# Normalisations taken in two chunks: centring, squares and sums chunk by chunk, in a one-core vision-transformer kernel

## The chip, the cores and the metric

One core of one Trainium2 chip runs the whole program in a single launch. The metric is the device time of that launch in microseconds; each kernel is run several times and the median is compared.

## The reference

The network is two small transformer layers over 16 images of 37 tokens (592 tokens) with 256 features. The kernel keeps everything transposed: features on the 128 partitions in C = 2 chunks, tokens along the free axis, in two halves of 296 tokens (HALF).

```python
def _layernorm(x, axis=-1, eps=1e-05):
    m = jnp.mean(x, axis=axis, keepdims=True)
    v = jnp.var(x, axis=axis, keepdims=True)
    return (x - m) / jnp.sqrt(v + eps)
...
h = _L0_tok_ref(...)                       # patch embedding
h = h + _L0_attn_ref(_layernorm(h), ...)   # two attentions, each behind an RMS norm
h = h + _L0_ffn_ref(_layernorm(h), ...)    # router, 32 experts, 2 shared experts
h = h + _L1_attn_ref(_layernorm(h), ...)   # third attention
h = h + _L1_ffn_ref(_layernorm(h), ...)    # int8-like FFN, scales from the largest |weight|
```

## The kernel before

There is no compiler scheduling: each engine (PE for matmuls, DVE for vector work, ACT for activations, POOL for GpSimd work, SP for DMA) has its own instruction list in the source and runs it strictly in order. Engines meet only at semaphores, so a wait holds everything behind it on that engine.

The norms are numbered. Norm 0 stands in front of the first attention, norm 1 (an RMS norm over the stream x0 of the first block) between the first and second attention, norm 2 in front of the experts, norm 3 in front of the third attention; the last one has code of its own.

Norms 0, 2 and 3 share one scheme. PE multiplies h by a matrix of 1/256 (two chunks summed in a PSUM bank, L1271 is the matmul helper) and gets the mean, each half in a bank. DVE subtracts it (`centre`, L887), one instruction for both chunks of a half. ACT squares xc (`norm`, L597), one instruction for a half, behind whatever stands ahead in its list. PE sums the squares into the variance (`norm`, L1271). ACT takes a table reciprocal root (L600) and squares it (L602). DVE corrects it with one Newton step and applies it (`norm_apply`: L896, L898, L901). POOL, in norms 0 and 1, multiplies by the norm's weights beside this (`norm_weighted`, L449). BUSY holds the numbers of filler matmuls (bf16, results unused) that PE issues ahead of the mean, between mean and variance, and after the variance.

Norm 1 is spread out. DVE adds the attention's output to x0 (`stream_added`, L992), ACT squares it (`stream_squares`, L607), PE sums it (`stream_variance`), ACT takes the root (`stream_rsqrt`, L612, L614), DVE does `norm_apply(1, ...)`. The first half goes in front of the second attention's projections. The second half is worked off inside `qk_units(1)`: this is a pipeline of six units (query and key projections of a half each), with the rotary products on DVE (rb L938, ra L941), their sum and scaling on POOL (L460, L464), head norms on PE and ACT (L658, L661), and the last product on DVE (L948, L952). On DVE the second half's `norm_apply` stands behind the rotary products of unit 0. On PE the projection of unit 3 waits for the second half of xn and for the rotary products of unit 0, whose PSUM bank it reuses.

In front of norm 2, SP loads the first four experts (L390) after the last attention scores, and ACT rounds each (L723, `high_part`) ahead of norm 2's squares in its list. DVE reads the largest weights of the last FFN in eight parts (`weight_peak`, L907) wherever it has time, the last of them and their combination (`weight_peaks`, L913) in front of `centre(2)`.

Of the kernel before, what the change touches and what calls it, by code (L numbers as in the profile page):

```python
# [11 lines left out]
P = 128  # L12
# [27 lines left out]
LN_EPS, RMS_EPS = 1e-5, 1e-6  # L40

START_BUSY = 19
BUSY = ((7, (0, 4, 14)), (0, (5, 0, 10)), (3, (0, 0, 8)), (7, (6, 4, 14)), (3, (5, 4, 10)))
LEAD = 3
ATTENTION_BUSY = 5

# [37 lines left out]
def program(nc, x, w_lin, consts, consts_bf, vecs, g_wq, g_down, g_k, g_v, g_wo, l_wq, l_wk, l_wv, l_wo,  # L84
# [4 lines left out]
    with ExitStack() as ctx:  # L89
# [169 lines left out]
        s_mean = sem("mean_summed")  # L259
        s_cent = sem("tokens_centred")  # L260
        s_sq = sem("squares_ready")
        s_var = sem("variance_summed")
        s_ars = sem("table_rsqrt_ready")
        s_xw = sem("tokens_weighted")
# [86 lines left out]
        def cent_count(n, hf):  # L351

            return 2 * {0: 0, 2: 1, 3: 2, 4: 3}[n] + hf + 1

        def score_bank(a, p):

            return 4 + 2 * (p % 2) if a < 2 else 6
# [73 lines left out]
        def _(pool):  # L431
# [8 lines left out]
            def norm_weighted(n, weight, factor):  # L440

                src = x0 if n == 1 else xc
                for hf in range(2):
                    if n == 1:
                        pool.wait_ge(s_x0, hf + 1)
                    else:
                        pool.wait_ge(s_cent, cent_count(n, hf))
                    for c in range(C):
                        ins = nc.gpsimd.tensor_scalar(xn[:, c, half(hf)], src[:, c, half(hf)],  # L449
                                                      weight[:, c:c + 1], -0.5 * factor, ALU.mult, ALU.mult)  # L450
                    ins.then_inc(s_xw, 1)
# [101 lines left out]
        def _(act_e):  # L553
# [29 lines left out]
                warmed[0] += 1  # L583
                nc.scalar.activation(spare[:, k:k + 1], eps[:, 0:1], func)  # L584

            def norm(n, mean=True, eps_at=0):

                if n != 2:
                    load_table(ACT.Abs_reciprocal_sqrt)
                for hf in range(2):  # L590
                    if mean:
                        act_e.wait_ge(s_cent, cent_count(n, hf))
                        src = xc
                    else:
                        act_e.wait_ge(s_x0, hf + 1)
                        src = x0
                    nc.scalar.activation(sq[:, :, half(hf)], src[:, :, half(hf)], ACT.Square).then_inc(s_sq, 1)  # L597
                for hf in range(2):
                    act_e.wait_ge(s_var, 2 * n + hf + 1)
                    link(nc.scalar.activation(ars[:, half(hf)], ps[2 + hf][:, 0:HALF], ACT.Abs_reciprocal_sqrt,  # L600
                                              bias=eps[:, eps_at:eps_at + 1]))
                    nc.scalar.activation(nt[:, half(hf)], ars[:, half(hf)], ACT.Square).then_inc(s_ars, 1)  # L602

            def stream_squares(hf):

                act_e.wait_ge(s_x0, hf + 1)
                nc.scalar.activation(sq[:, :, half(hf)], x0[:, :, half(hf)], ACT.Square).then_inc(s_sq, 1)  # L607

            def stream_rsqrt(hf):

# [261 lines left out]
        def _(dve):  # L872
# [11 lines left out]
            def centre(n):  # L884
                for hf in range(2):
                    dve.wait_ge(s_mean, cent_count(n, hf))
                    nc.vector.tensor_tensor(xc[:, :, half(hf)], h[:, :, half(hf)],  # L887
                                            bc(ps[hf][:, 0:HALF].unsqueeze(1), [P, C, HALF]), ALU.subtract)\
                        .then_inc(s_cent, 1)

            def norm_apply(n, count, eps_at=0, halves=range(2)):

# [32 lines left out]
            def qk_units(a):  # L925
                names = (("cos_g", "sin_g"), ("cos_l", "sin_l"))[a]
                cos, sin = (bc(const(x).unsqueeze(1), [P, HB, S]) for x in names)

                def images(ap):
                    return ap.rearrange("p (b s) -> p b s", s=S)  # L930

                for u in range(NPROJ + 1):
                    n = a * NPROJ + u
                    if u < NPROJ:
                        dve.wait_ge(s_swap, n + 1)
                        if n >= 2:
                            dve.wait_ge(s_rsum, n - 1)
                        nc.vector.tensor_tensor(images(rb[:, u % 2, :]), images(ps[5 + 2 * (u % 2)][:, 0:HALF]), sin,  # L938
                                                ALU.mult)
                        dve.wait_ge(s_qsq, n + 1)  # L940
                        nc.vector.tensor_tensor(images(ra[:, u % 2, :]), images(ps[PROJ_BANKS[u % 3]][:, 0:HALF]), cos,  # L941
                                                ALU.mult).then_inc(s_rope, 1)
                    if u >= 1:
                        w, k = u - 1, (u - 1) % 2
                        dve.wait_ge(s_qars2, n)

                        t = ps[MEAN_BANKS[w]][:, 0:HALF]
                        link(nc.vector.scalar_tensor_tensor(t, t, eps[:, 2:3], rs2[:, k, :], ALU.add, ALU.mult))  # L948
                        dve.wait_ge(s_rscaled, n)
                        j, hf = QK_UNITS[w]  # L950
                        dst = qt[:, j, half(hf)] if j < 2 else sq[:, 0, half(hf)]
                        ins = nc.vector.scalar_tensor_tensor(dst, t, -3.0, rt[:, k, :], ALU.add, ALU.mult)  # L952
                        ins.then_inc(s_qk, 1)
                    if u >= 2 and QK_UNITS[u - 2][0] == 2:

                        hf = QK_UNITS[u - 2][1]
                        for g in range(ACT_VARIANTS, 4):
                            ins = nc.vector.tensor_scalar(km[:, 0, g, half(hf)], sq[:, 0, half(hf)],  # L958
                                                          const("onehot4")[:, g:g + 1], None, ALU.mult)
                        ins.then_inc(s_kmv, 1)  # L960
                    if a == 1 and u == 0:
                        norm_apply(1, 4, 2, (1,))

            def normalise_grouped(a, p):

# [22 lines left out]
            def stream_added(hf):  # L988

                dve.wait_ge(s_wo, hf + 1)  # L990
                dve.wait_ge(s_x0s, hf + 1)
                nc.vector.tensor_tensor(x0[:, :, half(hf)], x0[:, :, half(hf)],  # L992
                                        psum[:, 2 - 2 * hf:4 - 2 * hf, 0:HALF], ALU.add).then_inc(s_x0, 1)

            nc.vector.memset(zeros[:], 0.0).then_inc(s_zero, 1)
            for k in range(KT):
# [25 lines left out]
            for a in range(2):  # L1022
# [21 lines left out]
                for hf in range(2):  # L1044
# [6 lines left out]
                    if hf == 0:  # L1051
                        weight_peak(1, 1)
                        weight_peak(1, 2)
                    else:
                        weight_peak(1, 3)
                        weight_peaks()


            centre(2)
            norm_apply(2, 6)  # L1060
            for hf in range(2):
                dve.wait_ge(s_xh, hf + 1)
# [206 lines left out]
        def _(pe):  # L1269
# [6 lines left out]
                for _ in range(count):  # L1276
                    mm(ps[bank][:, 0:HALF], lhsT, rhs, True, True)

            def norm(n, mean=True):

                spare_bank, busy = BUSY[n]
                if n:
                    keep_busy(spare_bank, busy[0])
                if mean:
                    for hf in range(2):
                        pe.wait_ge(s_h, cent_count(n, hf))
                        if n == 3:
                            pe.wait_ge(s_hd, hf + 1)
                        for c in range(C):
                            ins = mm(ps[hf][:, 0:HALF], const("mean"), h[:, c, half(hf)], c == 0, c == C - 1)  # L1290
                        ins.then_inc(s_mean, 1)
                    spare_bank = 7
                    keep_busy(spare_bank, busy[1])
                for hf in range(2):
                    pe.wait_ge(s_sq, 2 * n + hf + 1)
                    for c in range(C):
                        ins = mm(ps[2 + hf][:, 0:HALF], const("mean"), sq[:, c, half(hf)], c == 0, c == C - 1)
                    ins.then_inc(s_var, 1)
                keep_busy(spare_bank, busy[2])
# [43 lines left out]
            def qk_units(a):  # L1343
                projection(a, 0)
                for u in range(NPROJ):
# [5 lines left out]
                        pe.wait_ge(s_qk, a * NPROJ + 3)  # L1351
                        value_sums(a, 0)
                    if a == 1 and u == 0:
                        pe.wait_ge(s_x0, 2)
                        stream_variance(1)
                    exchange(a, u)
                    head_mean_squares(a, u)
# [108 lines left out]

            def stream_variance(hf):

                pe.wait_ge(s_sq, 2 + hf + 1)
                for c in range(C):  # L1470
                    ins = mm(ps[2 + hf][:, 0:HALF], const("mean"), sq[:, c, half(hf)], c == 0, c == C - 1)
                ins.then_inc(s_var, 1)

# [69 lines left out]
            def last_attention():  # L1543
# [25 lines left out]
                pe.wait_ge(s_cb, 2)  # L1569
                for m in range(C):  # L1570
                    mm(ps[4 + m][:, 0:HALF], const("ident"), xc[:, m, half(1)], True, False)
                pe.wait_ge(s_sq, 9)
                for c in range(C):
                    ins = mm(ps[6][:, 0:HALF], const("mean"), sq2[:, c, :], c == 0, c == C - 1)
                ins.then_inc(s_var, 1)
# [2 lines left out]
                for m in range(C):  # L1578
                    centred_projection(1, m, True)
                for c in range(C):  # L1580
                    pe.wait_ge(s_sq, 10 + c)
                    ins = mm(ps[7][:, 0:HALF], const("mean"), rs2[:, c, :], c == 0, c == C - 1)
                ins.then_inc(s_var, 1)
                plain_projection(0)
# [70 lines left out]
                for hf in range(2):  # L1655
                    mm(ps[2 * m + hf][:, 0:HALF], const("ident"), h[:, m, half(hf)], True, False)

            pe.wait_ge(s_cent, cent_count(2, 1))
            seed(0)
            pe.wait_ge(s_moe_w, 48)  # L1660
            pe.wait_ge(s_xn, 5)
# [270 lines left out]
```

## Time and profile before

| | us |
|---|---|
| median of 3 runs | 364.17 (363.68 to 365.55) |
| the profiled execution, whole | 365.47 |
| its span, first to last instruction | 363.6 |
| PE busy | 344.2 (95%) |
| DVE, ACT, POOL busy | 233.5, 196.1, 137.5 |

The span is the profile's; 1.87 us of the profiled execution lie around it. Each engine's busy time says how full it is on the whole; which of them sets the time at a place is read from the chain of work that ended last and from the idle time in front of an instruction.

### The profile page before, as it was taken

Reading aid. Unit: us, or ns where it says so; the run is one execution under the profiler, and the core shown is the slowest. Engines: PE = TensorE matmul, PEld = TensorE weight load, DVE = VectorE, ACT = ScalarE, POOL = GpSimd, SP = SyncE. Lnnn points to the kernel's source line nnn. Section 1 sums busy time; section 2 is a strip of 40 time slices with the busy share of each in tenths; the row PEclk is TensorE's granted clock in tenths of the full one; section 3 lists DMA queues with packets and bytes.
Section 4 is the critical chain, followed back from the end, with each engine's and each line's share of the span. In section 5 each row is a group of like instructions: output and inputs, shape, how many; then the busy total and the mean of one; then the engine's idle time right before and its main releaser. Section 6 shows DMA issues by size and latency. Waiting matters only on the chain.

```text
span 363.6 us, 9925 instructions
## 1 busy us (share of the span) xinstructions
PE 344.2 (95%) x3935; PEld 295.8 (81%) x3935; DVE 233.5 (64%) x512; ACT 196.1 (54%) x392; POOL 137.5 (38%) x145
## 2 busy tenths in 40 slices
PE   7999899898988999999999999999999999999994
PEld 6856667686657989999999999999999678676653
DVE  4656788897859466555555555555557464666687
ACT  5267943786464344445445444544543786425772
POOL 0046761472250256555666544444440002341000
PEclk9999999999989999999999999999999999999999
DMA  8930000000560244454444455444500000000001
GB/s 289 399 148 1 3 5 31 1 4 4 170 179 2 57 139 135 156 154 143 127 137 142 139 153 153 126 140 138 147 19 2 0 0 4 4 6 2 3 0 67
DMA packets 14865, 32.08 MB, mean 88 GB/s; under 512 B 2480, under 2 KB 4464, under 8 KB 14576
## 3 DMA queue, kind: packets, MB, share of 16 engines
q1 hardware_dynamic: 13328, 30.48, 26.6%
q10 hardware_dynamic: 1504, 1.13, 0.9%
q8 instruction: 24, 0.39, 0.4%
q14 instruction: 9, 0.07, 0.1%
HBM read 30.91 MB, written 0.69 MB: 87 GB/s over the span
## 4 chain that ended last, share of the span: by engine, by line
PE 76%; DVE 9%; ACT 8%; issue 2%; DMA 2%; ACTq 1%; SPq 1%; POOL 1%; DVEq 0%
PE psum L1271 76%; DMA km<-in_experts 2%; ACT L584 1%; DVE xn L901 1%; ACT region L855 1%; ACTq L563 1%; DVE km L1197 1%; ACT ah L744 1%; ACT region L679 1%; SPq L390 1%; DVE nt L898 1%; DVE nt L896 1%; ACT e L691 1%; ACT sq L597 1%; DVE rt L1126 1%
## 5 line engine op out<-in xcount | busy, mean ns | idle before, releaser
L1271 PE MATMUL psum<-xh,split_all 128*128 128x296 f32 x544 | 122.1, 299 | 0.0
L501 POOL TENSOR_TENSOR split_all<-km,split_all 128x768 fp32r<-128x768 f32 x34 | 62.6, 1844 | 81.3 <-ACT split_all L723 81.3
L1271 PEld LDWEIGHTS psum<-xh,split_all 128*128 128x128 f32 x544 | 91.6, 188 | 0.1
L1271 PE MATMUL psum<-xl,split_all 128*128 128x296 f32 (+1 forms) x288 | 85.4, 301 | 0.3 <-POOL xl L544 0.3
L744 ACT ACTIVATE ah<-rt 128x296 fp32r<-128x296 f32 x64 | 28.9, 452 | 72.7 <-DVE rt L1126 65.9
L1271 PEld LDWEIGHTS psum<-xl,split_all 128*128 128x128 f32 (+1 forms) x288 | 53.3, 187 | 1.2 <-issue 0.5
L1271 PE MATMUL psum<-ah,split_all 128*128 128x296 f32 x272 | 48.7, 300 | 1.7 <-ACT ah L744 1.6
L1128 DVE TENSOR_TENSOR al<-rt,ah 128x296 fp32r<-128x296 f32 x60 | 28.1, 468 | 31.0 <-ACT ah L744 31.0
L1123 DVE TENSOR_TENSOR rb<-psum,wb 128x296 f32<-128x296 f32 x60 | 28.0, 466 | 25.3 <-ACT psum L742 25.3
L1271 PEld LDWEIGHTS psum<-ah,split_all 128*128 128x128 f32 x272 | 40.6, 188 | 2.7 <-ACT ah L744 2.1
L1126 DVE TENSOR_TENSOR rt<-rb,psum 128x296 f32<-128x296 f32 x60 | 27.8, 463 | 4.8
L742 ACT ACTIVATE psum<-psum 128x296 f32<-128x296 f32 x60 | 24.1, 401 | 12.0 <-PE psum L1271 11.9
L723 ACT ACTIVATE split_all<-km 128x768 fp32r<-128x768 f32 x34 | 28.3, 833 | 3.8 <-DMA km<-in_experts 3.7
L1271 PE MATMUL psum<-al,split_all 128*128 128x296 f32 x136 | 30.0, 301 | 0.2
L691 ACT ACTIVATE e<-psum 101x592 f32<-101x592 f32 x24 | 15.7, 663 | 21.9 <-PE psum L1271 21.7
L544 POOL TENSOR_TENSOR xl<-mx,cst 128x592 fp32r<-128x592 f32 x8 | 9.6, 1202 | 45.0 <-DVE mx L1206 45.0
L1271 PEld LDWEIGHTS psum<-al,split_all 128*128 128x128 f32 x136 | 22.1, 189 | 0.9 <-POOL al L507 0.5
L1271 PE MATMUL psum<-cstb 128*128 128x296 bf16 (+1 forms) x174 | 21.4, 297 | 0.5 <-DVE km L958 0.3
L1271 PE MATMUL psum<-sq,cst 128*128 128x296 f32 x60 | 20.0, 453 | 1.9 <-ACT sq L597 1.8
L971 DVE RECIPROCAL rc<-psum 128x148 f32<-128x148 f32 x16 | 17.3, 1083 | 5.3 <-PE psum L1271 4.1
L1271 PEld LDWEIGHTS psum<-cstb 128*128 128x128 bf16 (+1 forms) x174 | 12.6, 100 | 8.7 <-issue 5.2
L1271 PEld LDWEIGHTS psum<-sq,cst 128*128 128x128 f32 x60 | 11.8, 204 | 6.8 <-ACT sq L597 3.5
(225 smaller groups left out, 578.6 us busy)
## 6 DMA issues: line engine op xcount, KB each, us to landing
km<-in_experts SPq DMA_DIRECT2D x34, 384.0 KB, 4.1
wb<-weights SPq DMA_DIRECT2D x32, 296.0 KB, 3.8
w_sb<-in_w SPq DMA_DIRECT2D x2, 1024.0 KB, 8.5
region<-in_x SPq DMA_DIRECT2D x6, 296.0 KB, 4.8
region<-in_w_lin ACTq DMA_DIRECT2D x6, 128.0 KB, 5.2
qkv_sb<-in_qkv_w SPq DMA_DIRECT2D x1, 768.0 KB, 4.8
cst<-in_consts SPq DMA_DIRECT2D x1, 502.5 KB, 7.1
out<-x SPq DMA_DIRECT2D x2, 148.0 KB, 1.8
```

The lines of the kernel that those rows point to most:

```text
L390: sp.dma_start(ring[i], experts[i, :, :]).then_inc(s_ring[i], 16)
L501: nc.gpsimd.tensor_tensor(wl[i], ring[i], wh[i].bitcast(f32), ALU.subtract)\
L544: nc.gpsimd.tensor_tensor(dg[:, p % 2, :, :], mx[:, p % 2, :].unsqueeze(2).broadcast_to([P, HEADS, S]), const("minus_ident").unsqueeze(1). ...
L691: nc.scalar.activation(e[0:ROWS, p % 2, 0:EC].rearrange("p (k n) -> p k n", k=2), psum[0:ROWS, sb0:sb0 + 2, 0:HALFPOS * S], ACT.Exp, scale ...
L723: nc.scalar.activation(wh[i], ring[i], ACT.Copy).then_inc(s_wsh, 1)
L742: nc.scalar.activation(gate, ps[bank][:, 0:HALF], ACT.Silu).then_inc(s_sg, 1)
L744: nc.scalar.activation(ah[:, j, :], act[:, j, :], ACT.Copy).then_inc(s_ah, 1)
L971: link(nc.vector.reciprocal(rc[:], bank[:, G4 * S:2 * G4 * S]))
L1123: nc.vector.tensor_tensor(gu[:, j, :], gate, weight, ALU.mult).then_inc(s_mulc, 1)
L1126: nc.vector.tensor_tensor(act[:, j, :], gu[:, j, :], ps[5][:, 0:HALF], ALU.mult).then_inc(s_act, 1)
L1128: nc.vector.tensor_tensor(al[:, j, :], act[:, j, :], ah[:, j, :].bitcast(f32), ALU.subtract)\
L1271: return nc.tensor.matmul(out_, lhsT, rhs, start=start, stop=stop, skip_group_check=True)
```

## The change

The centring, the squares and the sums of squares of norms 0, 2 and 3 are split by chunk: DVE issues two subtractions of 296 columns for each half and signals each; ACT squares each chunk as it is signalled, under a semaphore of its own; PE waits for each chunk ahead of its matmul. The same is done with the addition, squares and sums of norm 1. The POOL steps that read both chunks wait for the second. The fillers between mean and variance go from 4 to 2 in norms 0 and 3. The last `weight_peak` and `weight_peaks` go behind `centre(2)` on DVE. The second half's `norm_apply` of norm 1 goes in front of unit 0's rotary products on DVE. No arithmetic is changed.

```diff
-BUSY = ((7, (0, 4, 14)), (0, (5, 0, 10)), (3, (0, 0, 8)), (7, (6, 4, 14)), (3, (5, 4, 10)))
+BUSY = ((7, (0, 2, 14)), (0, (5, 0, 10)), (3, (0, 0, 8)), (7, (6, 2, 14)), (3, (5, 4, 10)))
...
+        def chunk_count(n, hf, c):
+            return C * (cent_count(n, hf) - 1) + c + 1
...
@@ norm_weighted, POOL
-                        pool.wait_ge(s_x0, hf + 1)
+                        pool.wait_ge(s_x0, C * (hf + 1))
-                        pool.wait_ge(s_cent, cent_count(n, hf))
+                        pool.wait_ge(s_cent, chunk_count(n, hf, C - 1))
...
@@ norm, ACT
-                    nc.scalar.activation(sq[:, :, half(hf)], src[:, :, half(hf)], ACT.Square).then_inc(s_sq, 1)
+                    for c in range(C):
+                        act_e.wait_ge(s_cent, chunk_count(n, hf, c))
+                        nc.scalar.activation(sq[:, c, half(hf)], xc[:, c, half(hf)], ACT.Square).then_inc(s_sqc, 1)
...
@@ stream_squares, ACT
-                act_e.wait_ge(s_x0, hf + 1)
-                nc.scalar.activation(sq[:, :, half(hf)], x0[:, :, half(hf)], ACT.Square).then_inc(s_sq, 1)
+                for c in range(C):
+                    act_e.wait_ge(s_x0, C * hf + c + 1)
+                    nc.scalar.activation(sq[:, c, half(hf)], x0[:, c, half(hf)], ACT.Square).then_inc(s_sq, 1)
...
@@ centre, DVE
-                    nc.vector.tensor_tensor(xc[:, :, half(hf)], h[:, :, half(hf)],
-                                            bc(ps[hf][:, 0:HALF].unsqueeze(1), [P, C, HALF]), ALU.subtract)\
-                        .then_inc(s_cent, 1)
+                    for c in range(C):
+                        nc.vector.tensor_tensor(xc[:, c, half(hf)], h[:, c, half(hf)], ps[hf][:, 0:HALF], ALU.subtract)\
+                            .then_inc(s_cent, 1)
...
@@ qk_units, DVE
+                    if a == 1 and u == 0:
+                        norm_apply(1, 4, 2, (1,))
                     if u < NPROJ:
                         dve.wait_ge(s_swap, n + 1)
...
-                    if a == 1 and u == 0:
-                        norm_apply(1, 4, 2, (1,))
...
@@ stream_added, DVE
-                nc.vector.tensor_tensor(x0[:, :, half(hf)], x0[:, :, half(hf)],
-                                        psum[:, 2 - 2 * hf:4 - 2 * hf, 0:HALF], ALU.add).then_inc(s_x0, 1)
+                for c in range(C):
+                    nc.vector.tensor_tensor(x0[:, c, half(hf)], x0[:, c, half(hf)], ps[2 - 2 * hf + c][:, 0:HALF], ALU.add)\
+                        .then_inc(s_x0, 1)
...
@@ end of the second attention, DVE
-                    else:
-                        weight_peak(1, 3)
-                        weight_peaks()
             centre(2)
+            weight_peak(1, 3)
+            weight_peaks()
             norm_apply(2, 6)
...
@@ norm, PE
                 for hf in range(2):
-                    pe.wait_ge(s_sq, 2 * n + hf + 1)
                     for c in range(C):
+                        pe.wait_ge(s_sqc, C * (cent_count(n, hf) - 1) + c + 1)
                         ins = mm(ps[2 + hf][:, 0:HALF], const("mean"), sq[:, c, half(hf)], c == 0, c == C - 1)
...
@@ stream_variance, PE
-                pe.wait_ge(s_sq, 2 + hf + 1)
                 for c in range(C):
+                    pe.wait_ge(s_sq, C * hf + c + 1)
```

## Rows read from the trace of the kernel before

**Rows 1.** The page: busy time of PE, and the chain's shares by engine

```profile
PE 344.2 (95%) x3935; PEld 295.8 (81%) x3935; DVE 233.5 (64%) x512; ACT 196.1 (54%) x392; POOL 137.5 (38%) x145
...
PE 76%; DVE 9%; ACT 8%; issue 2%; DMA 2%; ACTq 1%; SPq 1%; POOL 1%; DVEq 0%
```

**Rows 2.** Chain that ended last, whole span: start us, us, what

```profile
17.95 0.78 DVE xc L887
18.75 0.70 ACT sq L597
...
69.50 9.47 PE psum L1271 x92
...
95.45 6.13 DMA km<-in_experts
...
133.56 139.14 PE psum L1271 x1020
...
285.33 0.78 DVE xc L887
...
286.89 1.28 PE psum L1271 x4
```

**Rows 3.** Timeline, norm 0: start, us, engine, line, instruction, count [idle before]

```profile
18.74 0.67 PE L1271 MATMUL psum<-cstb 128*128 128x296 bf16 x4
...
19.50 2.26 PE L1271 MATMUL psum<-sq,cst 128*128 128x296 f32 x8
```

**Rows 4.** Timeline: pairs of 296-column instructions, on ACT and on DVE

```profile
5.49 0.77 ACT L574 ACTIVATE split_all<-region 128x296 fp32r<-128x296 f32 x2
...
96.78 0.83 DVE L1049 TENSOR_TENSOR h<-h,psum 128x296 f32<-128x296 f32 x2
```

**Rows 5.** Timeline, norm 1, weight loads of PE: the first half's sums

```profile
57.00 0.97 PEld L1271 LDWEIGHTS psum<-vec,outw_sb 128*128 128x128 f32 x8 [0.24 <-issue]
58.01 0.80 PEld L1271 LDWEIGHTS psum<-sq,cst 128*128 128x128 f32 x4
```

**Rows 6.** Timeline, second attention's first units: ACT, DVE, POOL and PE

```profile
66.08 0.47 DVE L938 TENSOR_TENSOR rb<-psum,cst 128x296 f32<-128x296 f32 x1 [1.38 <-PE psum L1271]
66.12 0.45 ACT L614 ACTIVATE nt<-ars 128x296 f32<-128x296 f32 x1
66.46 0.46 DVE L941 TENSOR_TENSOR ra<-psum,cst 128x296 f32<-128x296 f32 x1
67.00 0.82 POOL L460 TENSOR_TENSOR rt<-ra,rb 128x296 f32<-128x296 f32 x1 [2.99 <-DVE ra L941]
...
67.90 0.92 POOL L464 TENSOR_TENSOR rt<-rt,rs 128x296 f32<-128x296 f32 x1
68.18 1.27 DVE L901 TENSOR_TENSOR xn<-xn,nt 128x592 f32<-128x592 f32 x1
69.50 1.26 PE L1271 MATMUL psum<-xn,lk_sb 128*128 128x296 f32 x4 [0.97 <-DVE xn L901]
```

**Rows 7.** Timeline, norm 0's Newton step: first and last of three instructions

```profile
21.83 0.53 DVE L896 SCALAR_TENSOR_TENSOR nt<-psum,eps,nt 128x296 f32<-128x296 f32 x1 [2.11 <-ACT nt L602]
...
22.89 0.77 DVE L901 TENSOR_TENSOR xn<-xn,nt 128x592 f32<-128x592 f32 x1
```

**Rows 8.** Timeline, norm 2

```profile
100.66 1.79 ACT L723 ACTIVATE split_all<-km 128x768 fp32r<-128x768 f32 x2 [1.40 <-DMA km<-in_experts]
100.78 1.44 DVE L887 TENSOR_TENSOR xc<-h,psum 128x592 f32<-128x592 f32 x2
102.36 1.27 ACT L597 ACTIVATE sq<-xc 128x592 f32<-128x592 f32 x2
103.09 3.95 PE L1271 MATMUL psum<-sq,cst 128*128 128x296 f32 x8 [1.78 <-ACT sq L597]
```

**Rows 9.** Stretches of norm 2: us, busy times, granted clock, DMA share, GB/s

```profile
103.42:106.84 3.42, 3.42 (x8) 2.18 (x7) 0.60 (x2) 1.16 (x3) 1.74 (x1) 0.50 0.77 200
```

**Rows 10.** Timeline, PE: the longest idle time at full clock elsewhere

```profile
44.27 0.46 PE L1271 MATMUL psum<-e,region 101*32 101x74 f32 x16 [1.07 <-ACT e L691]
```

## What I predicted before the change was run

> **What bounds the kernel now.** I read the shares of busy time first: PE is at work for 344.2 us of a span of 363.6, and the chain that ended last runs over PE for 76% of it [rows 1]. So nearly every stretch is already PE's. What the change can win lies in the places where the chain leaves PE, and the second view is therefore the chain in order of time. It leaves PE in each norm. In norm 0 it goes from DVE's centring (0.78 us) to ACT's squares (0.70) and back to PE's sums at 19.50 [rows 2, 3], and in norm 3 in the same way [rows 2]. In norm 2 it comes from the DMA of the fourth expert (6.13 us) over ACT [rows 2, 8]. In norm 1 the first half's sums follow another PE job without a gap [rows 5], while the second half ends in a PE idle time of 0.97 us that DVE's xn ended [rows 6]. The third view is the timeline at those four places, to see for each engine what it was doing when its operand became ready. The fourth is the granted clock, because one stretch is not at full clock [rows 9].
>
> **Norm 0: chunks and two fillers fewer.** Now, PE starts summing squares at 19.50, which is 17.95 + 0.78 + 0.70 and hand-overs. No row shows the chunked instructions, so I take rows of the same shape: a pair of DVE instructions of 296 columns with a PSUM operand takes 0.83, so one is ready after 0.47 and the second is offset by 0.36; a pair of SBUF copies on ACT takes 0.77, so one takes 0.45 and the offset is 0.32 [rows 4, 6]. The first chunk is centred at 17.95 + 0.47 = 18.42, squared from 18.45 to 18.90, and PE could take it at 18.94. PE itself is then still at its fillers. Four of them occupied 18.74 to 19.41, of which the last 0.17 or so is the drain of the last, so that one fills about 0.125 [rows 3]; with two, the next matmul can be issued at 18.99. PE starts at 18.99 and not 19.50: 0.50 less. With four fillers left in, it would have been 19.24 and half that gain. The second chunk: centred by 17.95 + 0.83 = 18.78, squared by 19.26, wanted by PE half a half-sum later, at 19.49. It's in time. The second half's mean is read at 18.95, so its chunks are squared at about 19.90 and 20.22, and wanted at 19.99 and 20.49: PE goes through all eight pieces (2.26 us [rows 3]) without a gap. The whole 0.50 reaches the end, since the following root, Newton step and projection hang on these sums. Bounds: 0.25 (if PE's change from filler to sum takes the time of the two fillers) and 0.55 (both instructions cut to a chunk: 0.78 + 0.70 - 0.47 - 0.45 = 0.56). I take 0.50, because the PE slot is the later of the two.
>
> The costs of splitting are 0.06 on DVE for each half (0.83 against 0.77) and 0.07 on ACT (0.77 against 0.70) [rows 4, 8]. POOL's weighting waits for the second chunk and starts 0.06 later; its product is used two microseconds after it is done, so I cost it at nothing. If that cover were gone it would be the 0.06.
>
> The Trainium skill speaks against such a split: "VectorE: DVE Perf Modes", section "The TRN2 errata", says that instructions reading SBUF pay a fixed extra latency each, and advises tiles of at least 512 elements. By that rule all six halves of norms 0, 2 and 3 would pay 0.13 us, 0.8 in all, and the sum would be a gain of about 0.7. The trace agrees that a fixed cost exists (0.83 against 0.77), but the chain only waits for the first chunk.
>
> **Norm 3** repeats norm 0: from the start of the centring (285.33) to the first sum (286.89) it takes 1.56 [rows 2], where norm 0 takes 1.55, with the same instructions and the same four fillers. Gain 0.50, same bounds.
>
> **Norm 1, first half.** The squares would be ready about 0.55 earlier, but PE isn't. It loads weights for the output bias from 57.00 to 57.97 and starts the sums at 58.01 [rows 5]. The gain is the 0.04 between the two, called 0. The second half's squares are overtaken by PE's projections in the same manner. DVE's 0.06 goes into a wait for ACT. I cost this part at nothing; bounds -0.04 and +0.06.
>
> **Norm 1, Newton in front of unit 0.** Today DVE does rb and ra of unit 0 (66.08 to 66.92), then the Newton step, and xn is ready at 69.45, so that PE starts unit 3's projection at 69.50 [rows 6]. The last of its three instructions takes 1.27, against 0.77 in norm 0, and the three together 2.6 (66.83, behind ra, to 69.45) against 1.83 there (21.83 to 23.66) [rows 6, 7]. They ran while POOL did unit 0's sum and scaling (67.00 to 68.82), which ra released. Moved in front, the Newton step waits for ACT's root (66.12 + 0.45 = 66.57; this is the added wait, and unit 0's rb, which was ready at 66.08, is queued behind it). It then runs with POOL idle: 66.60 + 1.83 = 68.43. So xn is ready 1.02 earlier. But that isn't what PE gets, because the next wait is late: unit 3's projection also needs ra of unit 0, whose bank it takes. rb and ra follow at 68.35 and 68.72 and end at 69.18. PE starts at 69.22 and not 69.50: 0.28. Who else waits for the held rb? POOL's sum of unit 0 starts at 69.26 instead of 67.00, and POOL needs 0.9 + 0.9 for each unit. I followed the queues through: POOL ends unit 0 at 70.96, unit 1 at 72.75 (before 71.97), unit 2 at 74.53 (73.93), unit 3 at 76.32 (75.93). DVE's last product of unit 0 ends at 71.46 (71.14), of unit 1 at 73.25 (73.09), of unit 2 at 75.03, of unit 3 ahead of before. PE's head sums of unit 3 need unit 0's product, at 72.8, and those of unit 4 unit 1's, at 74.8. Each has more than a microsecond. From 69.50 on, the chain is PE's for 9.47 us [rows 2], so the 0.28 is carried. Bounds: 0 (POOL's delay reaches PE) and 0.35 (the hand-over shorter). A loss is bounded by the delay of DVE's product, 0.3.
>
> **Norm 2.** Here ACT is the gate, not DVE. Its two last expert roundings end at 102.45 and the squares follow at 102.36 (issue overlaps), while the centring was through at 101.5 and 102.22 [rows 8]. Moving the last weight peak behind the centring makes centring some 0.5 earlier and changes nothing, because ACT only comes when the fourth expert has landed at 101.58 [rows 2]. If the DMA were earlier in another run, the peaks' 0.7 would come in; I give this 0 to 0.2. The peaks themselves are wanted far later, after the fillers behind the sums. Chunking: first square ready at 102.36 + 0.45 + 0.04 = 102.85 where PE now starts at 103.09: 0.24. The expert loads start after the last scores and so move along with the gains ahead of them. Bounds 0 and 0.3, without the clock.
>
> **The sum.** 0.50 + 0 + 0.28 + 0.24 + 0.50 = 1.52 us. The profiled execution takes 365.47 (span 363.6 and 1.87 around it), so it would become 363.95. On the median of the runs, 364.17, the same 1.52 gives 362.65. The profiled execution is 1.3 slower than that median, and norm 2 has a reason for it, below. After norm 2, PE's stretch through the experts is one piece of the chain (139.14 us [rows 2]), so nothing there takes the gain back.
>
> **Rivals.**
> *The clock in norm 2.* In the trace PE's granted clock is 0.50 (1.2 instead of 2.4 GHz) from 103.42 to 106.84, behind an idle time of 1.78 us, and the eight pieces of the sums take 3.95 us where norm 0's take 2.26 [rows 3, 8, 9]: 1.69 us lost on the path. An idle time of 1.07 elsewhere was not followed by a fall [rows 10]. The change makes the idle time 1.54, between the two. If the clock then stays up, the profiled execution would end at 363.95 - 1.69 = 362.3, and a median that had the fall in it would come to about 361.0. The fastest run before, 363.68, is 1.79 below the profiled one, which is about one fall; so the fall is probably not in every run, and part of the median is free of it already. The Trainium skill, "TensorE: Matmul & The Clock Gate", section "What's actually happening", has it that the half rate is the default and activity releases it, and that the moment varies between runs. By that rule the shorter idle time would make falls rarer, and the trace agrees in direction. Time 361.4, chance 0.25.
> *The fillers were holding the clock.* Two fillers fewer in norms 0 and 3: PE is less active there, and the clock falls in one of them as it does in norm 2. Its price is up to 1.69 each, so 362.65 + 1.69 = 364.3 for one and 366.0 for both. This is slower than before. It decides as soon as one fall comes there; against it speaks that by my schedule PE is idle for only about 0.1 around the fillers. Chance 0.05.
> *The chunks pay nothing.* If the hand-over for each chunk costs more than the rows show (PE now waits four times instead of twice), or the fixed costs lie on the path, each norm gives 0.1 to 0.2: 364.17 - 0.28 - 0.5 = 363.4. Chance 0.13.
> *The unit pipeline takes the Newton gain back.* POOL begins unit 0 2.3 us later. If its backlog reached PE's head sums, norm 1 would lose up to 0.3 instead of gaining 0.28: 363.2. Chance 0.12.
> The forecast has the rest, 0.45. That the change does not do what it says is in the third rival.
>
> **How the numbers follow.** Forecast 362.6. The low end is the clock rival's, 361.0; the high end goes over the third and fourth rival and a fall kept in more runs, 364.0. A change of 0.5% is 1.82 us, about what a measurement of this kernel can tell from none. That bound is at 362.35, just 0.3 beyond the forecast, so the forecast's own chance is shared: of its 0.45 about a third lies beyond. Faster by over 0.5%: 0.15 + 0.25 = 0.40. Slower by over 0.5%: 0.03, from both falls. Within: 0.57.
>
> **What would show it.** Right: PE's first sum of squares 0.50 nearer to the start of the centring in norms 0 and 3, with no idle time among the eight pieces; xn L901 of the second half at 0.77 instead of 1.27 and PE's unit 3 released by ra L941, 0.28 nearer to the root; in norm 2 sums starting 0.4 us after the fourth rounding. Wrong: an idle time of PE between chunks; POOL as releaser inside units 3 to 5; a granted clock of 0.5 in norms 0 or 3; or the centring as the last releaser in norm 2.

## The result, and the profile after

The change took 2.0 us: median 362.10 us of 17 runs against 364.55 us of 17 runs of the kernel before on the same chips, ratio 0.9945 with a 95% interval of 0.9928 to 0.9962 (1.4 to 2.6 us). The 2.0 is taken from this ratio; the two medians by themselves differ by 2.45. The forecast was 362.6, a gain of 1.52. In a second set the same changed kernel gave 0.9939 [0.9916, 0.9962]. Single slow executions of the later sets (423 us and more: two of newton_only, one of after_busy2, one of the kernel before in each group) are left out of every ratio.

The profiled execution of the changed kernel took 360.44, its span is 358.6. That is 5.0 less than the span of before, more than twice the measured gain, so most of what two single traces differ by isn't the change. The page of the changed kernel, busy time by engine (here PE is as full as in [rows 1]):

```profile
span 358.6 us, 9933 instructions
PE 342.3 (95%) x3931; PEld 294.7 (82%) x3931; DVE 233.3 (65%) x520; ACT 197.1 (55%) x400; POOL 137.2 (38%) x145
```

Eight instructions more on DVE and eight more on ACT, four fewer on PE (two fillers in each of two norms). The chain that ended last, changed kernel (start us, us, what), at the places of [rows 2]:

```profile
19.12 0.47 DVE xc L890
19.62 0.82 ACT sq L598 x2
20.44 0.51 ACT ars L601
...
68.21 0.38 DVE ra L945
68.59 0.14 issue
68.73 9.44 PE psum L1273 x92
...
94.14 5.03 DMA km<-in_experts
99.19 0.84 ACT split_all L725
100.04 0.35 ACT sq L598
...
129.94 138.20 PE psum L1273 x1020
...
281.72 0.47 DVE xc L890
282.21 0.82 ACT sq L598 x2
```

In norms 0 and 3 the chain now goes from a centring of one chunk over ACT's squares straight to ACT's root: these are the squares of the second half, and the root of the first half stands behind them in ACT's list. PE's sums are no longer on it. Unit 3's projection is released by ra. Norm 2 still hangs on the DMA and ACT's rounding. The expert loop took 138.20 in this trace and 139.14 in [rows 2], though nothing in it was changed. Of the fourteen profiles this one and newton_only have 138.20, the other twelve 139.12 to 139.14; a second profile of the same changed kernel (after_again) has 139.12.

The timeline of norm 0 in the changed kernel, to be held against [rows 3]:

```profile
18.12 0.83 DVE L890 TENSOR_TENSOR xc<-h,psum 128x296 f32<-128x296 f32 x2 [0.67 <-PE psum L1273]
18.62 0.82 ACT L598 ACTIVATE sq<-xc 128x296 f32<-128x296 f32 x2 [5.12 <-DVE xc L890]
18.92 0.42 PE L1273 MATMUL psum<-cstb 128*128 128x296 bf16 x2
...
19.18 2.21 PE L1273 MATMUL psum<-sq,cst 128*128 128x296 f32 x8
```

The first sum starts 1.06 after the centring (1.55 before), and the eight pieces run without idle time. In norm 3 the same distance is 281.77 - 280.72 = 1.05.

To separate the change from what merely differs between executions, I cut all fourteen profiles of this study at the same instructions. The columns: norm 0's centring to the first projection; the bias job to norm 1's first projection; ACT's root to unit 3's projection; the first expert's DMA to norm 2's first sum; that sum to the expert loop; norm 3's centring to its projection. The last column is the stretch from there to the last FFN, in which no kernel differs. All are differences of starts, in us.

```
                    norm0  norm1  root-u3  load-sum2  sum2-loop  norm3  rest
before               5.86   5.31    3.92      9.99      30.47     5.77  52.02
newton_only          5.86   5.32    3.75      9.71      29.33     5.77  52.17
peaks_only           5.86   5.32    3.93      9.21      29.36     5.76  53.08
before_busy2         5.86   5.32    3.92      9.53      29.37     5.77  53.70
before_fillers2      5.86   5.31    3.92      9.51      29.36     5.78  52.72
after                5.31   5.20    3.75      8.81      29.51     5.22  52.16
after_again          5.30   5.20    3.75      8.67      29.60     5.21  52.45
chunks_only          5.30   5.32    3.91      9.35      29.50     5.21  52.18
after_fillers4       5.51   5.20    3.75      8.57      29.70     5.41  51.75
after_busy2          5.31   5.20    3.76      9.04      29.26     5.21  52.95
after_stream_back    5.30   5.31    3.75      8.80      29.37     5.21  52.47
after_peaks_back     5.31   5.20    3.75      8.64      29.71     5.21  51.63
after_newton_back    5.30   5.20    3.92      9.36      29.50     5.21  52.47
after_round_late     5.30   5.21    3.75      8.62      30.47     5.21  52.70
```

Four columns repeat to 0.02 and move only with their own part of the change. The others vary from one profile to the next, the last one by 2 us (51.63 to 53.70) over code that is the same in all. A gain of a tenth can be read in the first kind of column, while the medians can't show it.

### The profile page after: what moved, and what is told of

Its sections match the earlier page's. It is cut to its first block, busy times and chain, and to the rows that moved or that the text cites. A ratio compares the mean times of both kernels' runs of the same rounds, so it can differ in the third digit from the quotient of the medians.

```text
span 358.6 us, 9933 instructions
## 1 busy us (share of the span) xinstructions
PE 342.3 (95%) x3931; PEld 294.7 (82%) x3931; DVE 233.3 (65%) x520; ACT 197.1 (55%) x400; POOL 137.2 (38%) x145
## 4 chain that ended last, share of the span: by engine, by line
PE 78%; DVE 8%; ACT 8%; issue 2%; DMA 1%; ACTq 1%; SPq 1%; POOL 0%; DVEq 0%
PE psum L1273 78%; DMA km<-in_experts 1%; DVE xn L903 1%; ACT region L857 1%; DVE nt L898 1%; DVE nt L900 1%; ACTq L568 1%; ACT L589 1%; SPq L395 1%; DVE km L1199 1%; ACT region L681 1%; ACT e L693 1%; ACT sq L598 1%; DVE rt L1128 1%; ACT ah L746 1%
## 5 line engine op out<-in xcount | busy, mean ns | idle before, releaser
L1273 PE MATMUL psum<-cstb 128*128 128x296 bf16 (+1 forms) x170 | 20.6, 297 | 0.3 <-DVE km L962 0.3
L1273 PE MATMUL psum<-sq,cst 128*128 128x296 f32 x60 | 18.2, 417 | 0.3 <-ACT sq L598 0.3
L465 POOL TENSOR_TENSOR rt<-ra,rb 128x296 f32<-128x296 f32 x12 | 9.9, 825 | 15.1 <-DVE ra L945 15.1
```

The source lines that it names most:

```text
L465: nc.gpsimd.tensor_tensor(rt[:, u % 2, :], ra[:, u % 2, :], rb[:, u % 2, :], ALU.add)\
L1273: return nc.tensor.matmul(out_, lhsT, rhs, start=start, stop=stop, skip_group_check=True)
```

## The experiments

Each kernel was timed in five rounds beside the kernel before, in three groups, each on one chip: chunks_only, newton_only, peaks_only and after_fillers4; before_busy2, after_busy2, after_round_late and after_stream_back; after_again, after_peaks_back, after_newton_back and before_fillers2.

**chunks_only.** The change without norm 1's chunks, without the Newton move and without the move of the peaks:

```diff
-BUSY = ((7, (0, 4, 14)), ... (7, (6, 4, 14)), ...)
+BUSY = ((7, (0, 2, 14)), ... (7, (6, 2, 14)), ...)
 # centre, norm (ACT and PE) and norm_weighted by chunk, as in the change
```

> Of the change only the centring, squares and sums by chunk in norms 0, 2 and 3, with the two fillers fewer; norm 1, the Newton step and the weight peaks stay as before. My theory: PE's first sum of squares comes 0.5 us nearer to the start of the centring in norms 0 and 3 (from 1.55 to about 1.05), 0.24 nearer in norm 2; 1.2 to 1.3 us less in all, ratio about 0.9965, plus what the clock gives back in norm 2. Rival (the Newton step or the peaks carry much of the measured 2.0): this kernel gains under 0.8 us.

Measured: 0.9968 [0.9950, 0.9986], 1.2 us, as forecast. The interval runs from 0.5 to 1.8 us and so doesn't exclude the rival's 0.8 by itself; the table does it, with 0.56 for norm 0 and 0.56 for norm 3.

**newton_only.** The kernel before with `norm_apply(1, 4, 2, (1,))` in front of unit 0:

```diff
+                    if a == 1 and u == 0:
+                        norm_apply(1, 4, 2, (1,))
                     if u < NPROJ:
...
-                    if a == 1 and u == 0:
-                        norm_apply(1, 4, 2, (1,))
```

> Only the second half's Newton step of norm 1 moved in front of unit 0. My theory, corrected by the trace of the changed kernel: PE's projection of unit 3 starts 0.17 us nearer to ACT's root than before (3.75 instead of 3.92), released by ra and not by xn; no time that a median can show, ratio 0.9990 to 1.0000. Rival (the move carries the surplus of the measured gain): at least 0.5 us less, ratio under 0.9985.

Measured: 1.0007 [0.9984, 1.0030]; root to unit 3 is 3.75. The local gain is what was expected (the trace of the changed kernel had shown it already), and the interval can't resolve it. The rival's 0.5 us or more lies at its very edge.

**after_newton_back.** The same edit taken out of the changed kernel.

> The changed kernel with the second half's Newton step of norm 1 behind unit 0's rotary products again. Theory: PE's projection of unit 3 starts 3.92 after ACT's root instead of 3.75, 0.17 us in all, ratio 0.0005 above the changed kernel. Rival (the move carries the surplus of the measured gain over my sum): 0.5 us or more, ratio near 0.996.

Measured: 0.9958 [0.9934, 0.9981], with 0.9939 for the changed kernel in the same group, and 3.92 instead of 3.75. The difference of the ratios, 0.0019, would be 0.7 us, but either interval is wider than it. So whether more than the 0.17 hangs on the move is not settled here.

**peaks_only** and **after_peaks_back.** The move of the last peak done alone, and undone in the changed kernel:

```diff
-                    else:
-                        weight_peak(1, 3)
-                        weight_peaks()
             centre(2)
+            weight_peak(1, 3)
+            weight_peaks()
```

> Only the last weight peak and the combination of the peaks moved behind the centring of norm 2. My theory: the squares wait for ACT's expert roundings, so nothing changes, ratio 1.000 within 0.001. Rival: where the fourth expert lands earlier, the centring is what ACT waits for, and this gives up to 0.7 us, ratio down to 0.998.

> The changed kernel with the last weight peak and their combination in front of norm 2's centring again. Theory (the move gives nothing, since ACT comes late to the squares): same ratio as the changed kernel within 0.0015. Rival (beside chunked squares the centring is the gate once the fourth expert lands early, so the move pays only together with the chunks; in the profiles so far the fourth rounding ended 8.9 to 9.35 us after the first expert's DMA was issued in the four kernels with the peaks in front, and 8.2 to 8.6 after it in the five with them behind): 0.5 to 0.8 us slower than the changed kernel, ratio near 0.9965.

Measured: 1.0009 [0.9992, 1.0026] and 0.9935 [0.9911, 0.9958]. The medians show no gain of the move either way. The rival in the second expectation rested on a split I had seen in nine profiles: fourth rounding 8.9 to 9.35 after the first DMA's issue with the peaks in front, 8.2 to 8.6 with them behind. These two profiles break it. With the peaks in front the four roundings were done 7.70 after the issue (after_peaks_back):

```profile
96.63 3.73 ACT L725 ACTIVATE split_all<-km 128x768 fp32r<-128x768 f32 x4 [1.78 <-DMA km<-in_experts]
...
100.31 1.57 DVE L890 TENSOR_TENSOR xc<-h,psum 128x296 f32<-128x296 f32 x4
...
101.30 2.26 PE L1274 MATMUL psum<-sq,cst 128*128 128x296 f32 x8 [0.45 <-ACT sq L598]
```

and in after_newton_back, with them behind, 8.96. It was chance in nine traces. In after_peaks_back the centring (100.31) was in fact the last releaser, since the experts had landed early. That is the case I had priced at 0 to 0.2, and it does occur: the first sum comes 0.94 after the end of the fourth rounding (100.36 to 101.30), where it takes 0.40 in the changed kernel, so the peaks in front held this one execution by about 0.5. before_fillers2 shows the same, 1.23 instead of 0.64. In the four other profiles with the peaks in front the first sum follows the rounding as closely as elsewhere. How often the early landing comes is not known, so what the move is worth on average stays open.

**after_fillers4** and **before_fillers2.** The two fillers put back into the changed kernel, and taken out of the kernel before:

```diff
-BUSY = ((7, (0, 2, 14)), ... (7, (6, 2, 14)), ...)
+BUSY = ((7, (0, 4, 14)), ... (7, (6, 4, 14)), ...)
```

> The whole change, but with four fillers between mean and variance in norms 0 and 3, as before. My theory: PE's slot is 0.25 us later in each, so the first sum comes 1.30 after the start of the centring instead of 1.05, and 0.5 us of the gain is lost. Rival (fillers hold the clock): the granted clock in norms 0 and 3 differs between this kernel and the changed one.

> The kernel before with two fillers fewer between mean and variance in norms 0 and 3, squares unchunked. Theory (the squares are the last releaser there, so PE merely idles longer): first sum still 1.55 after the start of the centring, ratio 1.000 within 0.001. Rival (the fillers hold the clock): granted clock of 0.5 in norms 0 or 3 in the profile, up to 1.69 us slower for each, ratio up to 1.005 to 1.009.

Measured: 0.9958 [0.9936, 0.9981] and 0.9999 [0.9977, 1.0020]. Four fillers beside chunks (timeline of PE, after_fillers4):

```profile
19.19 0.67 PE L1273 MATMUL psum<-cstb 128*128 128x296 bf16 x4
19.70 2.15 PE L1273 MATMUL psum<-sq,cst 128*128 128x296 f32 x8
```

The centring began at 18.39, so the first sum comes after 1.31, as expected, and norms 0 and 3 take 5.51 and 5.41 instead of 5.31 and 5.21: each loses 0.2, not 0.25. The missing 0.05 lies at ACT's root. The first line is of after_fillers4, the second of the changed kernel:

```profile
20.90 0.51 ACT L601 ACTIVATE ars<-psum,eps 128x296 f32<-128x296 f32 x1 [0.19 <-PE psum L1273]
```

```profile
20.43 0.51 ACT L601 ACTIVATE ars<-psum,eps 128x296 f32<-128x296 f32 x1
```

With four fillers ACT waits 0.19 for PE's sum. With two it has no idle time: its squares of the second half end at 20.44 (19.62 + 0.82) and the root follows at once. So in the changed kernel ACT's own list is the next bound of norms 0 and 3, and fewer fillers still would bring nothing by these two traces. No run tests this.

Without chunks (before_fillers2) the fillers are free: 5.86 and 5.78 as before. PE's granted clock is full in that profile until PE's work is over, and of its 12 executions only 3 have a mean clock up to 0.995, against 12 of 34 of the kernel before beside it. The fillers were not what held the clock.

**before_busy2** and **after_busy2.** Eight fillers between mean and variance in norm 2:

```diff
-(3, (0, 0, 8))
+(3, (0, 8, 8))
```

> The kernel before with eight filler matmuls between mean and variance in norm 2 (PE has none there), so that PE is busy while ACT rounds the fourth expert. Fillers of 1.0 us fit in the idle time of 1.78. Theory (part of the gain is the clock, which falls in norm 2 behind the idle time in some runs and costs up to 1.69): no execution shows the granted clock of 0.5 in norm 2, and the mean falls by 0.3 to 0.8 us, ratio 0.998 to 0.999. Rival (the clock is no part of the gain): ratio 1.000.

> The changed kernel with the same eight fillers in norm 2. Theory (the change makes the idle time short enough, and the falls that remain lie in the shared expert, where they are hidden behind DVE's router): no further gain, ratio to the kernel before 0.9935 to 0.995, as for the change alone. Rival (falls still cost): up to 0.5 us more gain.

Measured: 1.0007 [0.9989, 1.0025] and 0.9935 [0.9915, 0.9954]. The first misses my expectation: its profile has no fall, but the mean didn't drop. (Three of the four other kernels of its kind have no fall in their profiles either, without these fillers.) The mean granted clock of an execution tells whether it had a fall: it is 0.992 to 0.995 in the seven profiles with one and 0.997 or more in the seven without. By this mark the fillers didn't remove all falls: 4 of the 12 executions of before_busy2 still have up to 0.995. Of the 33 executions of the kernel before in that group, the 15 with a mean clock up to 0.995 have a median of 364.37 and the 18 above it 364.49. In the first group the same two are 363.85 and 363.04 (17 each), in the third 364.43 (12) and 364.56 (22). For the changed kernel's 17 they are 362.10 (13 executions) and 362.06 (4). So the falls didn't become rarer with the change, and only in the first of three groups are the executions with a fall the slower ones. In after_busy2 the eight fillers were themselves in the way: the first sum comes 0.80 after the fourth rounding there, where it takes 0.40 in the changed kernel.

In a single trace the fall does cost something when it lies on the path: from norm 2's first sum to the expert loop the kernel before takes 30.47 with the fall among the sums [rows 9], and 29.33 to 29.37 in the four others of its kind. That is 1.1, not the 1.69 of my price. It is the only one of the fourteen profiles with a fall there, and the one with the longest idle time of PE in front of these sums (1.78; the others have 0 to 1.01). In the changed kernel the fall came later, in the first shared expert (stretches of the changed kernel; us, busy times, granted clock, DMA share, GB/s):

```profile
109.00:110.00 1.00, 1.00 (x6) 1.00 (x5) 0.98 (x15) 0.99 (x3) 0.00 (x0) 0.50 0.00 0
...
111.00:112.00 1.00, 1.00 (x5) 0.69 (x3) 0.86 (x5) 0.00 (x0) 0.00 (x0) 0.50 0.00 0
```

There PE has time to spare, because in the kernel before it waits 1.21 us for ACT's ah behind DVE's router at this place (first line, before). In the changed kernel the line has no idle time (second line):

```profile
117.19 0.82 PE L1271 MATMUL psum<-ah,split_all 128*128 128x296 f32 x4 [1.21 <-ACT ah L744]
```

```profile
113.85 0.70 PE L1273 MATMUL psum<-ah,split_all 128*128 128x296 f32 x4
```

Its sum2-loop of 29.51 is within the 29.26 to 29.71 of the chunked kernels without a fall.

**after_stream_back.** Norm 1's addition, squares and sums in one piece for each half again, in the changed kernel:

```diff
-                for c in range(C):
-                    nc.vector.tensor_tensor(x0[:, c, half(hf)], ...).then_inc(s_x0, 1)
+                nc.vector.tensor_tensor(x0[:, :, half(hf)], ...).then_inc(s_x0, 1)
```

> The changed kernel with norm 1's addition, squares and sums in one piece for a half, as before. Theory (PE is busy with the output bias and the projections when these are ready): no change to the changed kernel, PE's sums start at the same distance from the bias work, ratio to before 0.9935 to 0.9955. Rival (they carry part of the gain): 0.3 us or more slower than the changed kernel, ratio over 0.9955.

Measured: 0.9944 [0.9924, 0.9964]. But the norm 1 column goes from 5.20 to 5.31, so the chunks do give 0.11, where I had written 0 and bounded it at 0.06. PE's weight loads in the changed kernel, beside [rows 5]:

```profile
56.51 0.97 PEld L1273 LDWEIGHTS psum<-vec,outw_sb 128*128 128x128 f32 x8 [0.24 <-issue]
...
57.40 0.80 PEld L1273 LDWEIGHTS psum<-sq,cst 128*128 128x128 f32 x4
```

The sums' load starts 0.89 after the bias job and not 1.01, so it had been waiting for the squares after all, behind the end of a load that looked like its neighbour.

**after_round_late.** The changed kernel with the fourth expert's rounding behind norm 2's squares on ACT:

```diff
-            for i in range(NRING):
+            for i in range(NRING - 1):
                 high_part(i, i, 0, False)
             norm(2)
...
+                if n == 2:
+                    high_part(NRING - 1, NRING - 1, 0, False)
```

> The changed kernel with ACT's rounding of the fourth expert behind norm 2's squares instead of ahead of them. Theory (the landing of the fourth expert and its rounding gate the squares, 0.84 and the wait for the DMA): the squares start when the centring is done, 0 to 1.5 us earlier than now depending on the DMA, ratio to before 0.991 to 0.994, and with the centring as the last releaser the moved weight peaks begin to matter. Rival (the squares are no gate, or the late rounding holds the shared experts): ratio as for the change, 0.9945.

Measured: 0.9940 [0.9915, 0.9964], no better than the change. The timeline of after_round_late:

```profile
99.91 2.46 PE L1275 MATMUL psum<-sq,cst 128*128 128x296 f32 x8
...
101.33 0.83 ACT L727 ACTIVATE split_all<-km 128x768 fp32r<-128x768 f32 x1
...
102.06 0.49 ACT L603 ACTIVATE ars<-psum,eps 128x296 f32<-128x296 f32 x1
...
103.62 0.75 DVE L902 SCALAR_TENSOR_TENSOR nt<-nt,ars 128x296 f32<-128x296 f32 x1
```

The squares no longer wait for the fourth rounding, but the centring releases them no earlier: the first sum comes 8.62 after the first expert's DMA, where it takes 8.57 to 8.81 in five of the other chunked kernels. And the root took their place: it stands behind the rounding on ACT and starts 2.15 after the first sum, where it takes 1.30 in the changed kernel (100.43 to 101.73). And POOL's last subtraction, now later, ran beside DVE's Newton step (0.75 for L902, which reads two SBUF operands, against 0.47 in norm 0). The column behind it shows the loss, 30.47 against about 29.5. The 0.84 was not removed, only moved by one step along the same queue.

**after_again.** The changed kernel once more, as the mark of the last group.

> The changed kernel as it is, beside the two that take one part back, on one chip. All theories: ratio to before 0.9945 within 0.002; it is the mark for the next two.

Measured: 0.9939 [0.9916, 0.9962].

## Why the prediction was right

The sum of 1.52 lies inside the measured 1.4 to 2.6, near its low end. Term by term, by the table:

- **Norm 0, forecast 0.50: 0.55.** PE's slot after two fillers was the right releaser; start to first sum went from 1.55 to 1.06, as worked out. The other 0.05 comes after it: the root starts 1.25 after the first sum (19.18 to 20.43), where it took 1.30. It couldn't have come sooner, since ACT had the second half's squares in front of it.
- **Norm 3, forecast 0.50: 0.56.** The same, by the same rows.
- **Norm 1's chunks, forecast 0: 0.11.** The term was mis-sized, and 0.11 lies outside its bounds. I read two PE jobs next to each other as one bound by the other. The gap of 0.04 in the weight loads was a wait, not the end of the job ahead.
- **Newton in front, forecast 0.28: 0.17.** The mechanism is as described. The Newton step runs unstretched, xn is ready a microsecond earlier, ra becomes the releaser, and POOL's backlog never reaches PE: PE is busy for 9.44 from there, as before. The step that failed is the hand-over. I took 0.04 from ra's end to PE, as after xn. The chain shows 0.14 there (68.59 to 68.73). The rest of the schedule held to 0.1: DVE's last product of unit 0 waited for POOL and ended at 70.97, where I had 71.46, less the 0.60 by which this trace is ahead at the root. The timeline of the changed kernel at this place, to be held against [rows 6]:

```profile
67.06 0.77 DVE L903 TENSOR_TENSOR xn<-xn,nt 128x592 f32<-128x592 f32 x1
...
68.13 0.46 DVE L945 TENSOR_TENSOR ra<-psum,cst 128x296 f32<-128x296 f32 x1
...
68.73 1.24 PE L1273 MATMUL psum<-xn,lk_sb 128*128 128x296 f32 x4 [0.80 <-DVE ra L945]
...
70.50 0.47 DVE L956 SCALAR_TENSOR_TENSOR qt<-psum,rt 128x296 f32<-128x296 f32 x1 [0.72 <-POOL rt L469]
```

- **Norm 2, forecast 0.24: about 0.1.** The term is over-sized. From the end of the fourth rounding to the first sum it was 0.64 (102.45 to 103.09) and is 0.40 (100.03 to 100.43), as forecast. But the stretch behind it went from 29.35 to about 29.5. The Newton step moved forward into POOL's work: POOL splits experts until 103.60, and L900, which reads two SBUF tiles, takes 0.61 there against 0.47. I had used exactly this effect for norm 1 and did not look for it here. The other profiles bear it out: in the five kernels without chunks the same instruction (L898 there) takes 0.47. In the chunked ones (after_round_late aside) the stretch grows with it: 29.26 and 29.37 where it takes 0.47 or 0.48, 29.50 to 29.60 where 0.61 or 0.62, 29.70 and 29.71 where 0.80 and 0.84. The first two lines are of the changed kernel, the last one of newton_only, where POOL had ended at 104.58 and the instruction begins at 105.12:

```profile
98.23 5.37 POOL L506 TENSOR_TENSOR split_all<-km,split_all 128x768 fp32r<-128x768 f32 x3 [0.39 <-ACT split_all L725]
...
103.32 0.61 DVE L900 SCALAR_TENSOR_TENSOR nt<-nt,ars 128x296 f32<-128x296 f32 x1
```

```profile
105.12 0.47 DVE L898 SCALAR_TENSOR_TENSOR nt<-nt,ars 128x296 f32<-128x296 f32 x1
```

Together 0.55 + 0.56 + 0.11 + 0.17 + 0.1 = 1.5. That the sum agrees with the forecast to the tenth is luck: three terms were too small, by 0.05, 0.06 and 0.11, and two too large, by 0.11 and about 0.14.

**The rivals.** The clock rival was wrong in its size and its effect on the median: the falls didn't become rarer, the one that met the sums cost 1.1, and filling the idle time of the kernel before gave nothing (1.0007; by the low end of its interval, 0.9989, at most 0.4 us). That PE would idle 1.54 in front of these sums held for no profile: how long it idles there goes with the landing of the fourth expert, and in the changed kernel's trace it was 0.31. The reason I gave for part of the median, that the profiled execution of before was slow because of the fall, is true for 1.1 of that trace and not for the spread of the runs. "The fillers were holding the clock" is refuted by before_fillers2. "The chunks pay nothing" is refuted by chunks_only. The Trainium skill ("VectorE: DVE Perf Modes", section "The TRN2 errata") advises tiles of at least 512 elements. The traces agree that smaller ones cost more in all (the pairs of 296 take 0.83 and 0.82, against 0.77 and 0.70 for one instruction of 592), but at this place that stayed off the path, and the split paid. "The unit pipeline takes the gain back" is refuted by the columns of newton_only.

**What stays open.** The ratio gives 2.0, and 2.2 in the after_again group, where the columns account for 1.5. The difference is inside both intervals. If it is real, the one stretch that could hold it is from the first expert's DMA to norm 2's first sum: 9.59 on average over five kernels without chunks, 8.87 over nine with them, 0.7 apart where chunks explain 0.24. The traces place the rest: the fourth expert landed 7.96 after the first issue on average over the five and 7.48 over the nine, 0.48 apart, and from that landing to the first sum the means differ by 0.24. Single landings spread from 7.41 to 8.49 and from 6.83 to 8.10. The change edits none of these DMAs; whether its other effects make them land sooner is not shown. Among the chunked kernels the two with Newton behind are the longest (9.35, 9.36), but newton_only (9.71) is no shorter than its kind. No run tells a cause from chance here.

## What to carry to other kernels

Where one engine hands to the next in a chain of whole-tile steps, cut only the steps whose first part releases the next engine, and find the other release beside it: here 0.2 of each norm's 0.55 would have stayed behind two filler matmuls. Compare two traces by stretches cut at the same instructions, and trust those that repeat in kernels that share the code; the spans of two single executions differed by 5.0 us for a change worth 2.0. Before calling a step hidden, look at what the moved work will now run beside: an earlier Newton step met POOL's SBUF work and gave back 0.14 of the 0.24 that the stage had gained.

## What the runs showed of the hardware

A DVE instruction with two SBUF operands beside POOL's splitting waited for it. In the eight profiles in which POOL's instruction ran on for 0.15 or more after norm 2's L900 had begun, L900 ended 0.32 to 0.33 after POOL (in the changed kernel at 103.93, POOL at 103.60), and so took 0.48 to 0.84. In the other six, where POOL was done or all but done, it took 0.47.

The expert loop, 1020 matmul records without a change in any kernel, took either 139.12 to 139.14 or 138.20, with nothing between, in fourteen profiles, and both values for the same kernel.

PE's granted clock fell to 0.50 while PE had work in seven of the fourteen profiles: at 103.42 in the kernel before, and between 107.45 and 109.89 in six of the nine chunked kernels. The mean granted clock marks such a fall in about half of all executions, and it went with a longer time in one group of three.

Four experts of 384 KB, issued by the same instructions, had all landed between 6.83 and 8.49 after the first issue.
